# Criss-cross attention on one core: six of the 24 scan chunks move from the score pairs to the end of the head

## What is computed

```python
q = jnp.einsum('bchw,oc->bohw', x, Wq) + bq[None, :, None, None]      # 64 channels
k = jnp.einsum('bchw,oc->bohw', x, Wk) + bk[None, :, None, None]      # 64 channels
v = jnp.einsum('bchw,oc->bohw', x, Wv) + bv[None, :, None, None]      # 512 channels
eH = jnp.einsum('bchw,bcpw->bhwp', q, k)      # along the column, own pixel masked
eW = jnp.einsum('bchw,bchp->bhwp', q, k)      # along the row
att = jax.nn.softmax(jnp.concatenate([eH, eW], axis=3), axis=3)
outH = jnp.einsum('bcpw,bhwp->bchw', v, attH)
outW = jnp.einsum('bchp,bhwp->bchw', v, attW)
return gamma.reshape(()) * (outH + outW) + x
```

## Time and profile before

| | |
|---|---|
| median of 3 runs | 4426.95 us |
| profiled execution | 4430.1 us, span 4428.3 us |
| mean granted clock of TensorE in it | 0.86 |
| busy: PE, DVE, ACT, POOL | 80%, 58%, 42%, 28% of the span |
| DMA | 266 GB/s over the span |

### The profile page before, as it was taken

How to read it: one execution, slowest core, us unless ns; L and a number is a source line. 1 busy time by engine, 2 the same in 40 slices (tenths; PEclk the granted TensorE clock), 3 DMA queues, 4 the chain that set the end, 5 groups by cost and what they waited for, 6 DMA issues and landing times.

```text
span 4428.3 us, 97049 instructions
## 1 busy us (share of the span) xinstructions
PE 3545.5 (80%) x33624; PEld 2431.6 (55%) x33624; DVE 2586.0 (58%) x3802; ACT 1875.7 (42%) x3852; POOL 1246.6 (28%) x1075
## 2 busy tenths in 40 slices
PE   3987978778887887878977798878988778884865
PEld 1544755456564564645655466554755456563755
DVE  6546764477554774538745576455765477554643
ACT  1545634165241752427532474325634165242621
POOL 0000341404413044220433214240241404413333
PEclk9998799888898798997999879889799888996665
DMA  7958688986989779996899968899689986999399
GB/s 273 297 187 276 209 275 263 326 279 197 312 259 315 255 200 307 289 315 224 240 303 310 302 206 257 273 325 292 208 272 268 330 280 194 316 261 286 96 288 287
DMA packets 824051, 1179.35 MB, mean 266 GB/s; under 512 B 56560, under 2 KB 574192, under 8 KB 823536
## 3 DMA queue, kind: packets, MB, share of 16 engines
q1 hardware_dynamic: 509136, 831.94, 61.5%
q10 hardware_dynamic: 314400, 340.86, 24.0%
HBM read 832.83 MB, written 339.74 MB: 265 GB/s over the span
## 4 chain that ended last, share of the span: by engine, by line
issue 33%; DMA 26%; PE 21%; POOL 10%; DVE 4%; SPq 3%; ACT 2%; ACTq 1%; POOLq 0%; DVEq 0%
DMA xr<-x 23%; POOL acc L496 4%; PE banks L1033 4%; PE banks L1034 4%; PE banks L1035 4%; POOL prob_col L486 4%; PE banks L1107 3%; PE banks L1109 2%; PE banks L1108 2%; DMA v_in<-v_pixel_major 2%; POOL qk_pair L468 2%; SPq L377 1%; DVE floor L770 1%; PE banks L1085 1%; DMA x_first<-x 1%
## 5 line engine op out<-in xcount | busy, mean ns | idle before, releaser
L1033 PE MATMUL banks<-wv_hi,x_hi 128*128 128x512 f16 x2304 | 936.2, 406 | 247.9 <-DVE x_lo L804 247.8
L812 DVE SCALAR_TENSOR_TENSOR v_out<-banks,proj,v_out 128x512 f16<-128x512 f32 x576 | 431.2, 749 | 1076.7 <-ACT v_out L591 1075.8
L496 POOL TENSOR_TENSOR acc<-acc,xr 128x768 f32<-128x768 f32 x384 | 716.3, 1866 | 878.0 <-DMA xr<-x 700.5
L1034 PE MATMUL banks<-wv_lo,x_hi 128*128 128x512 f16 x2304 | 930.1, 404 | 0.0
L1035 PE MATMUL banks<-wv_hi,x_lo 128*128 128x512 f16 x2304 | 924.5, 401 | 0.0
L591 ACT ACTIVATE v_out<-banks,proj 128x512 f16<-128x512 f32 x576 | 390.8, 684 | 970.3 <-PE banks L1035 968.9
L468 POOL TENSOR_TENSOR qk_pair<-qk_f,qk_pair 128x256 f16<-128x256 f32 x288 | 202.6, 703 | 2034.4 <-ACT qk_pair L607 2027.2
L1107 PE MATMUL banks<-prob_row,v_in 96*128 96x96 f16 x3072 | 475.0, 217 | 309.9 <-DMA v_in<-v_pixel_major 259.9
L893 DVE SCALAR_TENSOR_TENSOR acc<-banks,att,acc 128x384 f32<-128x384 f32 x768 | 443.1, 609 | 266.6 <-PE banks L1109 265.9
L1033 PEld LDWEIGHTS banks<-wv_hi,x_hi 128*128 128x128 f16 x2304 | 237.6, 103 | 519.7 <-issue 314.7
L1107 PEld LDWEIGHTS banks<-prob_row,v_in 96*128 96x128 f16 x3072 | 318.8, 104 | 367.0 <-issue 229.6
(11 more groups left out here) (104 smaller groups left out, 7055.4 us busy)
## 6 DMA issues: line engine op xcount, KB each, us to landing
v_in<-v_pixel_major SPq DMA_DIRECT2D x768, 384.0 KB, 7.1
x_raw<-x ACTq DMA_DIRECT2D x290, 512.0 KB, 6.9
x_next<-x SPq DMA_DIRECT2D x384, 384.0 KB, 3.7
v_pixel_major<-v_out ACTq DMA_DIRECT2D x576, 256.0 KB, 4.0
xr<-x SPq DMA_DIRECT2D x384, 384.0 KB, 9.5
out<-acc SPq DMA_DIRECT2D x384, 384.0 KB, 8.6
qk_halves<-qk_pair ACTq DMA_DIRECT2D x288, 128.0 KB, 4.1
x_first<-x SPq DMA_DIRECT2D x24, 768.0 KB, 9.0
```

The source lines that it names most:

```text
L496: nc.gpsimd.tensor_tensor(acc[tt][:, px], acc[tt][:, px], xr[n % XR][:, :], ALU.add).then_inc(res_added, 1)
L812: nc.vector.scalar_tensor_tensor(out=v_out[tile % V_OUT][:, :, 1, :], in0=bank[tile % 2][:, :].rearrange("p (t c) -> p t c", t=CT), scalar ...
L1033: nc.tensor.matmul(dst, s_hi, m_hi, start=(t == 0), stop=False)
L1034: nc.tensor.matmul(dst, s_hi, m_lo, start=False, stop=False)
```

## The change

A new constant EARLY = 6. `scan_at_head(k)` gives chunk k - 14 to the head items 14 to 19, and `scan_at_pair(p)` deals the other 18 chunks over the 24 pairs: none at pair 0, 4, 8, ..., one at each other. ACT and DVE see the chunks in these places. SP's loop is written differently, but issues the same loads in the same order as before.

```diff
+    EARLY = 6
...
+        def scan_at_head(k):
+            return range(k - HEAD + EARLY, k - HEAD + EARLY + 1) if k >= HEAD - EARLY else range(0)
+
         def scan_at_pair(p):
-            return range(p * SCAN // PAIRS, (p + 1) * SCAN // PAIRS)
+            left = SCAN - EARLY
+            return range(EARLY + p * left // PAIRS, EARLY + (p + 1) * left // PAIRS)
...
-                for p in range(PAIRS):
-                    if items:
-                        for c in scan_at_pair(p):
-                            if c + NXT < SCAN:
-                                load_next((b + 2) % B, b + 1, c + NXT)
+                if items:
+                    for c in range(NXT, SCAN):
+                        load_next((b + 2) % B, b + 1, c)
...
                 for k in range(HEAD):
                     if items:
                         item(b + 1, k)
+                        for c in scan_at_head(k):
+                            if c % 2 == 1:
+                                see_next(b + 1, c)
...
                 for k in range(HEAD):
                     if items:
                         item(b + 1, k)
+                        for c in scan_at_head(k):
+                            if c % 2 == 0:
+                                see_next(b + 1, c)
```

## The result

The changed kernel takes 4510.08 us, the median of 4 runs (4500.98 to 4513.65); the kernel before, 4429.26 us with one run more than above. The ratio of the two is put at 1.0202, with a 95% interval of 1.0155 to 1.025; the medians alone give 1.0182: some 81 us slower, 2%. The forecast was 4492 us, slower, in a range of 4425 to 4555.

What follows compares the result with a forecast made beforehand. The bound changes by stage: full DMA engines at the head's end, DVE beside row pairs, PE beside column pairs. Head cost 96 us less 31 from the pairs gave +65 on 4430.1, forecast 4492 us, range 4425 to 4555.

Steps and rivals of the forecast that it cites:

- The first wait: Head, behind item 14: chunk 0 lands 9.8 us after SP's first issue; with its scan 11.5 us.
- The rounds: Head: two buffers make chunks 2 and 4 wait their turn; chunk 0's issue to pair 0 takes 31.0 us, before 15.6.
- chunk 2's round: Head, second round: issues 1.0 us, landing taken as 8; with the scan 10.7 us.
- The last round: Head, chunk 4: issue and landing in a by now quiet queue, 1.0 + 4.1 us, then the scan, 1.7.
- turn 0: Head of the first turn: chunk 0 is already there, only the two later rounds stick out, about 4 us.
- The 28 us: Head: by ring order chunk 2 cannot start ahead of four v loads; its round some 4 us longer, about 28 more.
- The pairs' part: Row and column pairs, with fewer scans, give back 4.5 us a turn, 31 us over 7 turns.
- The term that was too small: Row pairs: ACT's two fewer scans count only where DVE waits for ACT; half of 3.3, so 1.65 us a turn.
- The column pairs: Column pairs: DVE two scans fewer, ACT one, but PE leaves only 2.2 us in 40; taken as 1.2.
- The one of no change: Head and pairs: rounds are short and the pairs give 9.9 us a turn; about 4433 us, chance 0.18.
- The gaps that swallow the scans: Head: scans fill DVE's 6.8 us gaps at no cost; faster, 4395 to 4377 us, chance 0.05.
- PE's clock: Row pairs: head gaps may leave PE at 1.2 GHz, 7.5 us a turn, +52; 4544 us, chance 0.13.

Runs made afterwards that it cites:

- e4: As e3, with the loads of chunks 0 and 1 also issued ahead of the 48 loads of q and k; ratio to the kernel before 1.0067.
- e3: The changed kernel with the four first loads of v issued behind the load of chunk 11; ratio to the kernel before 1.0123.
- e7: The changed kernel with six buffers for the six early chunks, all loaded in a row behind q and k; ratio to the kernel before 1.0077.
- e8: As e7, with the early chunks' loads ahead of q and k and the first v loads behind chunk 11; ratio to the kernel before 1.0021.
- e6: The changed kernel with chunks 0 to 5 neither loaded nor scanned, the other 18 beside the pairs; ratio to the kernel before 0.9951.
- e12: Against the kernel before: chunks 0 to 2 in own buffers behind item 17, 9 chunks at row pairs, 12 at column pairs, v loads last; ratio 1.0069.

## Why the prediction was right

**The first wait: right.** Chunk 0 is issued after item 14 has ended, and DVE stands still until it lands. Predicted 11.7 us of waiting in the turn shown (1970.7 to 1982.4), measured 14.86, and 11.2 to 14.9 over turns 1 to 6. The way from SP's issue to the scan was 10.1 us, predicted 9.8; the rest is that item 14 ended 4.7 us ahead of the issue and not 2.0.

**The rounds: right, and somewhat too short.** From SP's issue of chunk 0 to pair 0 I had 31.0 us. It was 32.9 in the turn shown and 32.8 to 35.5 over turns 1 to 6, mean 33.6. Before the change the same way was 15.4 us in the mean, forecast 15.6. Nearly all of the difference lies in chunk 2's round: over turns 1 to 6 DVE's second scan started 13.0 us behind the first, where I had 10.7. In the turn shown chunk 2 took 10.4 us from issue to scan (1999.46 to 2009.87) where I had 9.0: the landings were 8.2 to 9.9, and I had taken 8, a choice between 4.1 and 15 that happened to lie near. The last round was as forecast in length (landing 3.2 to 3.7; 7.0 us from scan to scan, forecast 6.8), but not in kind: DVE had no third wait for a chunk, it waited 4.04 us for ACT's `v_out` behind chunk 3 and came to chunk 4 when that had landed. Together the head costs 17.9 us a turn and not 15.4, and 7.1 in turn 0, not 4. This is the mis-sized term: 6 x 2.5 + 3 = 18 us too little, of which the pairs took back 7 x 0.4 = 3; 81 us were measured, 65 forecast.

That the waits for chunks are a cause beside the bytes is shown by e4 (same bytes as e3, 25 us less), e7 (same bytes, 4 us a turn less in the head than e3) and e8 (same bytes, no wait, 12 us a turn less than after the change). The 6 us a turn that e8 keeps are there without a wait, so the moved bytes or the scans themselves may have a part in the loss that my chain of rounds does not name. That the v loads ahead of chunk 2 made its round long is shown by e3: 6.50 us of waiting became 1.21.

The prediction cites the Trainium skill ("DMA: Bandwidth & Descriptors", section on queues, rings and completion order) for the rule that a DMA engine takes a queue's descriptors in ring order. The trace agrees: chunk 2 landed 0.5 us behind the last v load, and in 3.5 to 4.2 us with the v loads away. The 28 us that this rule would have added to my sum stand beside 22 us (profiled spans) to 35 us (ratios) that e3 took away.

**The pairs' part: right in sum, wrong in its parts.** Forecast 4.5 us a turn, measured 4.9, and 6.0 in e6. That the sum came out is luck in part: one term was too small and the other too large. The row pairs gave 4.6 (5.8 in e6) and not 3.3. The term that was too small is ACT's: DVE's waits for ACT's `v_out` there, 4.7 us a turn before the change, are gone altogether, where I had counted 1.65; DVE's waits for PE grew from 0.7 to 3.1. The column pairs gave 0.3 (0.2 in e6) and not 1.2: PE's 2.2 us of slack in 40 was no slack of the scans' making.

**The rivals.** The one of no change needed a way of under 26.5 us from chunk 0's issue to pair 0; it was 33.6. The gaps that swallow the scans are e8: no scan there waits for its chunk, but the head grows by about as much as the pairs give. PE's clock: it fell to 0.68 in the head's end, where other waits hid the slow matmuls, but it was 0.91 in the row pairs, 0.89 before (0.88 and 0.87 in the mean over turns 1 to 6); it did not come down beside the pairs. Nothing behind the pairs caught up: the rest of a turn is 374.1 us, 373.8 before.

## What to carry to other kernels

An engine that idles is not free for work whose data has yet to come: ask when the transfer is issued, what is ahead of it in its queue, and how many rounds of load, use and release fit into the gap. With two buffers a second chunk can't be had sooner than one round after the first, so moving three uses per buffer in front of a critical step puts two rounds in front of it. And when a stage with full DMA engines gets longer, waits and bytes can both be behind it: here the same bytes took 64 to 70 us, by the order of the loads and the number of buffers. Before you read a run in which a transfer was moved out of a stage, count from its trace how many bytes really left: most of a load that is issued near the end of a stage may not have been in it.

## What the runs showed of the hardware that was not expected

- A load lands late behind others in the same queue: the 384 KB loads of chunks 2 and 3 took 8.2 to 9.9 us behind four v loads, those of chunks 4 and 5 took 3.2 to 3.7 us in the empty queue (after).
- With the DMA engines at a share of 0.94 to 0.99 over the whole head in every kernel, 20.7 to 20.9 MB took 70.2, 66.0, 65.2 and 63.9 us (e3, e7, e4, e8): a share near 1 did not fix the time.
- Beside the column pairs PE is granted 0.50 to 0.52 of its clock (1.2 GHz) in each window shown, though it is busy nine tenths of the time (40.5 of 44.5 us in e6); these pairs took 44.4 to 44.8 us with nine scans or twelve, as long as the chunks came in time.
- Nine scans beside the row pairs took 48.6 us in one order (e6) and 55.3 in another (e12); the granted clock in the turns shown was 0.94 and 0.84. Cause and effect are not separated.
